# Moving a chain of projections one slot later behind an engine's PSUM read-out, with a per-channel weight folded into a scan's input

## Chip, cores and metric

One NeuronCore of a Trainium2 chip runs the whole program. The metric is device time in microseconds (us) of one execution; the kernel before was timed three times (median 1166.73 us, 1166.54 to 1167.99) and once more under the hardware profiler.

## What is computed

Input x is 8 samples of 512 tokens by 256 channels. Each sample goes through two residual layers.

Layer 0, per sample (all scans run over the tokens, from state 0):

```python
ctx   = ema(x, tau_ctx)                                  # h = alpha*h + x_t
wg    = sigmoid(concat(x, ctx) @ Wg.T + bg);  gated = x * wg
mod   = 0.5 + sigmoid(gelu(x @ Wn1.T + bn1) @ Wn2.T + bn2)      # 8 values a token
traces_d = ema(gated * mod[..., d], tau_d)               # d = 0..7
temporal = sum_d traces_d * blend_w[d]                   # blend_w: 8 x 256, a softmax over d
gate  = sigmoid(temporal @ Wtemp.T + btemp);  soma = gelu(x @ Wsoma.T + bsoma)
x     = x + layernorm((soma * gate) @ Wout.T) * gamma + beta
```

Layer 1 is a mixture: three shared feed-forward networks (256 to 1024 to 256 with relu) and two expert networks picked by a type index, added with weights from a small gate, and the residual.

## The kernel before

**Slots.** Activations are kept as 128 channels by 512 tokens, two tiles for 256 channels. Every fp32 product is three matmuls of rounded and remainder parts (lines 588 to 592). The work of a sample's mixture is 5 networks of 8 hidden tiles, 40 *slots*. In slot k TensorE does `up(k+2)` (6 matmuls, one hidden tile two slots ahead), then `down(k)` (6 matmuls, that tile's share of the network's output in the two banks `ps_down`). ScalarE does `relu(k+2)` (`hid_hi`, line 864), VectorE `relu_lo(k+2)` (`hid_lo`, line 1068). `down(k)` waits for `hid_lo` of tile k. When a network ends (slots 8, 16, 24, 32) ScalarE reads `ps_down` out first (`read_out`, lines 866 to 877, two ACTIVATEs to `y`), and the first `down` of the next network waits for it.

**Beside the mixture** of sample b, layer 0 of sample b+1 is computed. Which step stands where is written by hand in `PLAN_TENSOR`, `PLAN_SCALAR`, `PLAN_VECTOR` and `PLAN_SYNC` (lines 47 to 67): a step at slot k is issued ahead of that slot's mixture work on its engine, a step at k + 0.5 behind it; so on one engine k + 0.5 and k + 1 are the same place, if the step there is alone. Each engine works through its queue in order; semaphores tie the queues together. The plans are for mixtures 0 to 6 (mixture 0 has its own plan up to slot 7); mixture 7 has no layer 0 beside it.

**The traces** are on VectorE. `ema_in{d}` (slot 7.5 + 2d, lines 1157 to 1172) writes `trace = (modb + 0.5) * gates` for both channel tiles and scans tile 0; `ema_out{d}` (slot 8.5 + 2d, lines 1173 to 1185) scans tile 1 and adds both, times `blend_w`, to `temporal` (for d = 0 a TENSOR_SCALAR writes `temporal`). The last, `ema_out7`, is at slot 22.5.

**The context chain behind them**: `temp_hi` on ScalarE (slot 23.5, waits for the last sum) and `temp_lo` on VectorE (24) split `temporal`; `tgate` is 12 matmuls on TensorE (24.5) and two sigmoids on ScalarE (25); `sg`, `sg_hi`, `sg_lo` multiply by `soma` and split; `out` is 24 short matmuls (27.5); `ln_stats`, `ln_sqrt`, `ln_norm` normalize; `turn` transposes on TensorE (31.5) and ScalarE reads it out (32.5); `x2`, `x2_hi`, `x2_lo` (33 to 34.5) make the next mixture's input. SyncE loads the next x into `xt` at slot 33, once `x2` has used the old one.

**Others.** `mod` is a sigmoid of 8 x 512 on ScalarE (line 916) with a `nop` behind it that raises `mod_ready`; SyncE stores it to DRAM and loads it back as a broadcast (`modb`). `shared_gate_part` is six VectorE instructions of 256 elements at slot 33 (`GATE_PART_SLOT`). In mixture 0 and a few slots of mixture 1, weights are still being split: ScalarE rounds (`wi_round`, `wo_round`, `tile_round`, line 833), GpSimd subtracts (lines 1473, 1478, 1484), SyncE loads and stores the parts (`load_tile`, `keep_tile`, lines 450 to 462), all in the order of the same slots.

```python
                elif step == "temp_hi":
                    act.wait_ge(ema_sum, (n - 1) * (2 * D) + 2 * D)
                    hi(both(ct_hi), both(temporal)).then_inc(temp_hi_ready, 1)
```

Of the kernel before, what the change touches and what calls it, by code (L numbers as in the profile page):

```python
# [7 lines left out]
ALU = mybir.AluOpType  # L8
ACT = mybir.ActivationFunctionType
# [5 lines left out]
P = 128  # L15
B, T, E = 8, 512, 256
CT = E // P
D = 8
# [27 lines left out]

PLAN_TENSOR = {
    0.5: ["mod_hidden"], 1.5: ["soma"], 2.5: ["mod", "gate_hidden"], 4.5: ["wgate"],
    24.5: ["tgate"], 27.5: ["out"], 31.5: ["turn"],
}  # L50
PLAN_SCALAR = {
    1: ["mod_hidden"], 2: ["soma"], 3: ["mod"], 4: ["gate_exp"], 5: ["wgate"],
    23.5: ["temp_hi"], 25: ["tgate"], 26: ["sg_hi"], 29: ["ln_sqrt"], 32.5: ["turn"], 34: ["x2_hi"],
    36: ["next_x_hi"], 38.5: ["next_ctx_hi"],
}
PLAN_VECTOR = {
    0.5: ["gate_part"], 1.5: ["mod_hidden_lo"], 3.5: ["gate_logits"],
    4.5: ["gate_soft", "mix1", "mix2"], 5.5: ["mix3"], 6: ["gated"], 6.5: ["mix0"],
    24: ["temp_lo"], 25.5: ["sg"], 26: ["sg_lo"], 28.5: ["ln_stats"], 29.5: ["ln_norm"], 33: ["x2"], 34.5: ["x2_lo"],
    36.5: ["next_x_lo"], 37: ["next_ctx_scan"], 39: ["next_ctx_lo"],  # L60
}
for _d in range(D):
    PLAN_VECTOR[7.5 + 2 * _d] = [f"ema_in{_d}"]
    PLAN_VECTOR[8.5 + 2 * _d] = [f"ema_out{_d}"]
PLAN_SYNC = {
    3: ["mod"], 4: ["modb0", "modb1"], 8: ["store"], 10: ["modb2"], 14: ["modb3"], 33: ["next_x"],
}
PLANS = {"sync": PLAN_SYNC, "tensor": PLAN_TENSOR, "scalar": PLAN_SCALAR, "vector": PLAN_VECTOR, "gpsimd": {}}

# [18 lines left out]
FILLERS = {"x": 10, "out": 3, "normed1": 2, "x2": 7, "gate": 5, "mix": 20}  # L88
OPEN_SPREAD = 2
OPEN_VECTOR_INPUTS = {0: 0, 1: 1, 4: 3, 6: 5}  # L90
GATE_PART_SLOT = 33
MIX_ORDER = (1, 2, 3, 0)
HALF = T // 2
FINAL_OWN = P
# [39 lines left out]
def build(nc, x, w_ctx, params, types_row, types_all, shared_wi, shared_wo, expert_wi, expert_wo,  # L134
# [5 lines left out]
    with ExitStack() as ctx:  # L140
# [3 lines left out]
        def sem(name):  # L144
            return ctx.enter_context(nc.semaphore(name))
# [38 lines left out]
        mod = sb("mod", [D, T])  # L184
        modb = sb("modb", [P, 2, 2, T])
# [3 lines left out]
        alpha = sb("alpha", [P, D + 1])  # L189
        blend_w = sb("blend_w", [P, CT, D])  # L190
# [71 lines left out]
        mod_ready = sem("mod_ready")  # L262
# [568 lines left out]
        def _(act):  # L831
# [62 lines left out]
            def beside(step, k, p):  # L894
                n, f = p.n, p.f
                if step in ("x_hi", "next_x_hi"):
                    m = n + (step == "next_x_hi")
                    act.wait_ge(x_loaded, m * 16 + 16)
                    hi(both(xg_hi), both(xt)).then_inc(x_hi_ready, 1)
                elif step in ("ctx_hi", "next_ctx_hi"):  # L900
                    m = n + (step == "next_ctx_hi")
                    act.wait_ge(ctx_ready, m * 2 + 2)
                    hi(both(ct_hi), both(ctxt)).then_inc(ctx_hi_ready, 1)
                elif step == "soma":
                    for c in range(CT):
                        act.wait_ge(aux_ready[c], p.aux[c]["soma"] + 1)
                        act.activation(soma[:, c, :], ps_aux[c][:, :], ACT.Gelu, bias=col(C_BSOMA, c))\
                            .then_inc(aux_free[c], 1)
                elif step == "mod_hidden":
                    act.wait_ge(aux_ready[0], p.aux[0]["mod_hidden"] + 1)  # L910
                    act.activation(modh[:, :], ps_aux[0][:, :], ACT.Gelu, bias=col(C_BN1)).then_inc(aux_free[0], 1)
                    act.wait_ge(aux_free[0], p.aux[0]["mod_hidden"] + 1)
                    hi(modh_hi[:, :], modh[:, :]).then_inc(modh_hi_ready, 1)
                elif step == "mod":
                    act.wait_ge(aux_ready[1], p.aux[1]["mod"] + 1)
                    act.activation(mod[:, :], ps_aux[1][0:D, :], ACT.Sigmoid, bias=par[0:D, C_BN2:C_BN2 + 1])\
                        .then_inc(aux_free[1], 1)
                    act.wait_ge(aux_free[1], p.aux[1]["mod"] + 1)
                    act.nop().then_inc(mod_ready, 1)
                elif step in ("wgate", "tgate"):  # L920
                    bias = {"wgate": C_BG, "tgate": C_BTEMP}[step]
                    for c in range(CT):
                        act.wait_ge(aux_ready[c], p.aux[c][step] + 1)
                        act.activation(gates[:, c, :], ps_aux[c][:, :], ACT.Sigmoid, bias=col(bias, c))\  # L924
                            .then_inc(aux_free[c], 1)
# [3 lines that stand above are left out]
                elif step == "sg_hi":  # L929
                    act.wait_ge(sg_ready, (n - 1) * 2 + 2)  # L930
                    hi(both(xg_hi), both(gates)).then_inc(sg_hi_ready, 1)
                elif step == "ln_sqrt":
                    act.wait_ge(meanvar_ready, n)
                    act.activation(std[:, :], meanvar[:, :, 1], ACT.Sqrt, bias=eps[:, :]).then_inc(std_ready, 1)
                elif step == "turn":

                    if later((n - 1) * 16):
                        act.wait_ge(out_stored, (n - 1) * 16)
                    for c in range(CT):
                        act.wait_ge(aux_ready[c], p.aux[c]["turn"] + 1)  # L940
# [117 lines left out]
        def _(dve):  # L1058
# [38 lines left out]
            def mixture(b, k, parity, last):  # L1097
# [22 lines left out]
            def final_mix(parity):  # L1120
# [10 lines left out]
                dve.tensor_tensor(x2[:, parity, 1, FINAL_OWN:T], ps_aux[1][:, FINAL_OWN:T], x2[:, parity, 1, FINAL_OWN:T],  # L1131
                                  ALU.add).then_inc(final_added, 1)

            def beside(step, k, p):
                n, f = p.n, p.f
                if step in ("x_lo", "next_x_lo"):
# [20 lines left out]
                elif step.startswith("ema_in"):  # L1157

                    d = int(step[-1])
# [4 lines left out]
                    for c in range(CT):  # L1164
                        if d:

                            dve.wait_ge(ema_sum, (n - 1) * (2 * D) + (2 * d - 1 + c))
                        dve.scalar_tensor_tensor(trace[:, c, :], modb[:, d // 2 % 2, d % 2, :], 0.5, gates[:, c, :],  # L1168
                                                 ALU.add, ALU.mult).then_inc(ema_in, 1)
                    dve.wait_ge(ema_in, (n - 1) * (2 * D) + (2 * d + 1))  # L1170
                    dve.tensor_tensor_scan(trace[:, 0, :], alpha[:, d:d + 1].broadcast_to([P, T]), trace[:, 0, :], 0.0,  # L1171
                                           ALU.mult, ALU.add).then_inc(ema_trace, 1)
                elif step.startswith("ema_out"):
                    d = int(step[-1])
                    dve.wait_ge(ema_in, (n - 1) * (2 * D) + (2 * d + 2))
                    dve.tensor_tensor_scan(trace[:, 1, :], alpha[:, d:d + 1].broadcast_to([P, T]), trace[:, 1, :], 0.0,  # L1176
                                           ALU.mult, ALU.add).then_inc(ema_trace, 1)
                    for c in range(CT):
                        dve.wait_ge(ema_trace, (n - 1) * (2 * D) + (2 * d + 1 + c))
                        if d == 0:  # L1180
                            last = dve.tensor_scalar(temporal[:, c, :], trace[:, c, :], blend_w[:, c, 0:1], None, ALU.mult)
                        else:
                            last = dve.scalar_tensor_tensor(temporal[:, c, :], trace[:, c, :], blend_w[:, c, d:d + 1],  # L1183
                                                            temporal[:, c, :], ALU.mult, ALU.add)
                        last.then_inc(ema_sum, 1)
                elif step == "temp_lo":
                    dve.wait_ge(temp_hi_ready, n)
                    lo(both(ct_lo), both(temporal), both(ct_hi)).then_inc(temp_split, 1)
# [7 lines left out]
                elif step == "ln_stats":  # L1196
# [6 lines left out]
                    for t in range(TT):  # L1203
                        last = dve.bn_aggr(meanvar[:, t, :], stats[:, t, :])
# [386 lines left out]
```

## Time and profile before

| | |
|---|---|
| median of 3 runs | 1166.73 us |
| the profiled execution's own time | 1168.23 us |
| its span (first to last instruction) | 1166.2 us |
| TensorE busy | 1093.4 us, 94% |
| VectorE busy | 798.5 us, 68% |
| ScalarE busy | 410.6 us, 35% |
| GpSimd busy | 121.0 us, 10% |
| mean granted TensorE clock | 0.969 of full |

PE is TensorE, DVE VectorE, ACT ScalarE, POOL GpSimd, SPq the queue on which SyncE issues DMAs. In rows of the timeline the first number is the start in us from the span's start, the second the time from the start to the end of the piece, "x2" the instructions merged in it, and a bracket the idle time of the engine before it with what ended it. A row of a group by form has its busy time in us and the mean of one in ns. Busy time of PE holds overlap (a matmul of 512 columns shows about 0.39 us and the next starts 0.23 us after it), so what TensorE loses is read from starts and waits, not from the share.

### The profile page before, as it was taken

The page shows a single profiled execution, that of the slowest core. Times are in us where ns is not written, and L with a number is a line of the kernel's source. Part 1 is how long each engine was busy: PE and PEld are TensorE (multiplying, and loading weights), DVE is VectorE, ACT ScalarE, POOL GpSimd, SP SyncE. Part 2 cuts the span into 40 slices and gives each one's busy share as a digit, 9 for nine tenths or more (in the row PEclk, how much of TensorE's full clock was granted, in tenths as well). Part 3 has the DMA queues.
Part 4 walks back from the last instruction along what each step waited for, and adds up shares of the span by engine and source line. Part 5 has one row for each costly group of instructions (what it writes and reads, how often), then busy time and mean ns, then how long its engine had stood idle before and what let it go on. Part 6 is the DMA issues. An engine that isn't in the chain of part 4 may idle for free.

```text
span 1166.2 us, 12367 instructions
## 1 busy us (share of the span) xinstructions
PE 1093.4 (94%) x4706; PEld 869.8 (75%) x4706; DVE 798.5 (68%) x1223; ACT 410.6 (35%) x638; POOL 121.0 (10%) x50
## 2 busy tenths in 40 slices
PE   7699677989889999999999999999999999999998
PEld 5177456768678887888878887788878888788886
DVE  7975996638965589465975589465975589545225
ACT  7155333643224422343233422343233422332221
POOL 2814445512000000000000000000000000000000
PEclk9599988989999999999999999999999999999999
DMA  5058794478835546354645456354644465455550
GB/s 213 5 198 291 282 347 150 179 285 279 311 136 194 181 181 234 112 201 181 230 144 198 180 182 219 124 198 173 243 145 164 176 218 201 144 180 199 206 179 30
DMA packets 37772, 224.30 MB, mean 192 GB/s; under 512 B 4498, under 2 KB 4754, under 8 KB 16082
## 3 DMA queue, kind: packets, MB, share of 16 engines
q1 hardware_dynamic: 37714, 223.52, 53.2%
q8 instruction: 37, 0.61, 0.2%
q14 instruction: 21, 0.17, 0.0%
HBM read 189.82 MB, written 33.69 MB: 192 GB/s over the span
## 4 chain that ended last, share of the span: by engine, by line
PE 59%; DVE 33%; DMA 3%; issue 2%; ACT 2%; SPq 0%; DVEq 0%; ACTq 0%
PE ps_down L590 8%; PE ps_up L590 8%; PE ps_down L592 8%; PE ps_up L592 8%; PE ps_up L591 8%; PE ps_down L591 8%; DVE trace L1168 6%; DVE temporal L1183 5%; DVE hid_lo L1068 5%; DVE trace L1176 5%; DVE trace L1171 5%; PE ps_aux L590 3%; PE ps_aux L591 3%; PE ps_aux L592 3%; DMA split_wi<-ex 2%
## 5 line engine op out<-in xcount | busy, mean ns | idle before, releaser
L1068 DVE SCALAR_TENSOR_TENSOR hid_lo<-ps_up,hid_hi 128x512 fp32r<-128x512 f32 x320 | 219.5, 687 | 330.8 <-ACT hid_hi L864 329.5
L864 ACT ACTIVATE hid_hi<-ps_up 128x512 fp32r<-128x512 f32 x320 | 191.6, 599 | 495.7 <-PE ps_up L592 495.4
L590 PE MATMUL ps_down<-hid_hi,wo 128*128 128x512 f32 x640 | 257.7, 403 | 40.4 <-ACT y L876 22.7
L590 PE MATMUL ps_up<-x_hi,wi 128*128 128x512 f32 (+1 forms) x644 | 257.1, 399 | 3.0 <-DMA wi<-split_wi 2.9
L592 PE MATMUL ps_down<-hid_hi,wo 128*128 128x512 f32 x640 | 254.5, 398 | 0.0
L592 PE MATMUL ps_up<-x_hi,wi 128*128 128x512 f32 (+1 forms) x644 | 253.2, 393 | 0.0
L591 PE MATMUL ps_up<-x_lo,wi 128*128 128x512 f32 (+1 forms) x644 | 253.2, 393 | 0.0
L591 PE MATMUL ps_down<-hid_lo,wo 128*128 128x512 f32 x640 | 251.4, 393 | 0.0
L590 PEld LDWEIGHTS ps_down<-hid_hi,wo 128*128 128x128 f32 x640 | 120.9, 189 | 74.2 <-issue 30.0
L590 PEld LDWEIGHTS ps_up<-x_hi,wi 128*128 128x128 f32 x644 | 121.5, 189 | 30.5 <-DMA wi<-split_wi 3.8
L592 PEld LDWEIGHTS ps_down<-hid_hi,wo 128*128 128x128 f32 x640 | 121.2, 189 | 29.8
L592 PEld LDWEIGHTS ps_up<-x_hi,wi 128*128 128x128 f32 x644 | 122.2, 190 | 28.4
L591 PEld LDWEIGHTS ps_down<-hid_lo,wo 128*128 128x128 f32 x640 | 121.5, 190 | 27.7
L591 PEld LDWEIGHTS ps_up<-x_lo,wi 128*128 128x128 f32 x644 | 122.0, 189 | 26.5
L1183 DVE SCALAR_TENSOR_TENSOR temporal<-trace,blend_w,temporal 128x512 f32<-128x512 f32 x98 | 82.9, 891 | 0.0
L1168 DVE SCALAR_TENSOR_TENSOR trace<-modb,gates 128x512 f32<-128x512 f32 x112 | 77.2, 733 | 0.0
L1176 DVE TENSOR_TENSOR_SCAN trace<-alpha,trace 128x512 f32<-128x512 f32 x56 | 73.4, 1310 | 0.0
L1171 DVE TENSOR_TENSOR_SCAN trace<-alpha,trace 128x512 f32<-128x512 f32 x56 | 70.7, 1262 | 0.0
L1484 POOL TENSOR_TENSOR ex<-ex 128x1024 fp32r<-128x1024 f32 x16 | 41.5, 2597 | 79.2 <-ACT ex L833 79.2
L1117 DVE SCALAR_TENSOR_TENSOR x<-y,g,x 128x512 f32<-128x512 f32 x56 | 41.0, 785 | 0.2
L924 ACT ACTIVATE gates<-ps_aux,par 128x512 f32<-128x512 f32 x28 | 19.3, 689 | 61.5 <-PE ps_aux L592 61.5
L1478 POOL TENSOR_TENSOR wo<-raw_wo,wo 128x1024 fp32r<-128x1024 f32 x10 | 27.7, 2771 | 55.2 <-ACT wo L833 55.2
(197 smaller groups left out, 1004.3 us busy)
## 6 DMA issues: line engine op xcount, KB each, us to landing
wi<-split_wi SPq DMA_DIRECT2D x70, 1024.0 KB, 4.9
wo<-split_wo SPq DMA_DIRECT2D x70, 1024.0 KB, 4.8
modb<-mod_scratch SPq DMA_DIRECT2D x28, 512.0 KB, 4.5
split_wi<-ex SPq DMA_DIRECT2D x8, 1024.0 KB, 8.7
split_wo<-ex SPq DMA_DIRECT2D x8, 1024.0 KB, 9.3
split_wi<-wi SPq DMA_DIRECT2D x6, 1024.0 KB, 7.5
split_wo<-wo SPq DMA_DIRECT2D x6, 1024.0 KB, 8.3
xt<-in_x SPq DMA_DIRECT2D x8, 512.0 KB, 3.6
```

The source lines that it names most:

```text
L590: pe.matmul(ps, w_hi, x_hi, start=start, stop=False)
L591: pe.matmul(ps, w_hi, x_lo, start=False, stop=False)
L592: return pe.matmul(ps, w_lo, x_hi, start=False, stop=stop)
L864: act.activation(hid_hi[:, k % NU, :], ps_up[k % NU][:, :], ACT.Relu).then_inc(hid_hi_ready, 1)
L1068: dve.scalar_tensor_tensor(hid_lo[:, k % NU, :], ps_up[k % NU][:, :], 0.0, f32(hid_hi[:, k % NU, :]), ALU.max, ALU.subtract).then_inc(hid_ ...
L1117: dve.scalar_tensor_tensor(x2[:, parity, c, :], y[:, y_at(i, parity), c, :], g[:, i:i + 1], x2[:, parity, c, :], ALU.mult, ALU.add).then_i ...
L1168: dve.scalar_tensor_tensor(trace[:, c, :], modb[:, d // 2 % 2, d % 2, :], 0.5, gates[:, c, :], ALU.add, ALU.mult).then_inc(ema_in, 1)
L1171: dve.tensor_tensor_scan(trace[:, 0, :], alpha[:, d:d + 1].broadcast_to([P, T]), trace[:, 0, :], 0.0, ALU.mult, ALU.add).then_inc(ema_trac ...
L1176: dve.tensor_tensor_scan(trace[:, 1, :], alpha[:, d:d + 1].broadcast_to([P, T]), trace[:, 1, :], 0.0, ALU.mult, ALU.add).then_inc(ema_trac ...
L1183: last = dve.scalar_tensor_tensor(temporal[:, c, :], trace[:, c, :], blend_w[:, c, d:d + 1], temporal[:, c, :], ALU.mult, ALU.add)
L1478: pool.tensor_tensor(wo_lo[:, u % 2, :], raw_wo[:, u % 2, :], f32(wo_hi[:, u % 2, :]), ALU.subtract)\
L1484: pool.tensor_tensor(ex[:, j % 2, 1, :].bitcast(F32R), ex[:, j % 2, 1, :], ex[:, j % 2, 0, :], ALU.subtract)\
```

## The change

- The chain from `temp_hi` to `x2_lo` is moved back by a half to a whole slot in the four plans; `next_x` by one slot; `GATE_PART_SLOT` from 33 to 31.
- The 0.5 is added to `mod` by a second ScalarE instruction (in place of the `nop`); `ema_in` multiplies `modb` by the column of `blend_w` and by `gates`, so that what is scanned is already weighted.
- `ema_out` adds by TENSOR_TENSOR. For d = 0 the product is written into `temporal` and scanned there, and the two TENSOR_SCALARs are gone.

```diff
-    24.5: ["tgate"], 27.5: ["out"], 31.5: ["turn"],
+    25.5: ["tgate"], 28.5: ["out"], 32: ["turn"],
 PLAN_SCALAR
-    23.5: ["temp_hi"], 25: ["tgate"], 26: ["sg_hi"], 29: ["ln_sqrt"], 32.5: ["turn"], 34: ["x2_hi"],
+    24.5: ["temp_hi"], 26: ["tgate"], 27: ["sg_hi"], 29.5: ["ln_sqrt"], 33: ["turn"], 34.5: ["x2_hi"],
 PLAN_VECTOR
-    24: ["temp_lo"], 25.5: ["sg"], 26: ["sg_lo"], 28.5: ["ln_stats"], 29.5: ["ln_norm"], 33: ["x2"], 34.5: ["x2_lo"],
+    24.5: ["temp_lo"], 26.5: ["sg"], 27: ["sg_lo"], 29: ["ln_stats"], 30: ["ln_norm"], 33.5: ["x2"], 35: ["x2_lo"],
 PLAN_SYNC
-    3: ["mod"], 4: ["modb0", "modb1"], 8: ["store"], 10: ["modb2"], 14: ["modb3"], 33: ["next_x"],
+    3: ["mod"], 4: ["modb0", "modb1"], 8: ["store"], 10: ["modb2"], 14: ["modb3"], 34: ["next_x"],
-GATE_PART_SLOT = 33
+GATE_PART_SLOT = 31
-                    act.nop().then_inc(mod_ready, 1)
+                    act.activation(mod[:, :], mod[:, :], ACT.Copy, bias=0.5).then_inc(mod_ready, 1)
+            def trace_of(d):
+                return trace if d else temporal
+            def ema_scan(n, d, c):
+                dve.wait_ge(ema_in, (n - 1) * (2 * D) + (2 * d + 1 + c))
+                scan = dve.tensor_tensor_scan(trace_of(d)[:, c, :], alpha[:, d:d + 1].broadcast_to([P, T]), trace_of(d)[:, c, :],
+                                              0.0, ALU.mult, ALU.add)
+                scan.then_inc(ema_trace if d else ema_sum, 1)
-                        dve.scalar_tensor_tensor(trace[:, c, :], modb[:, d // 2 % 2, d % 2, :], 0.5, gates[:, c, :],
-                                                 ALU.add, ALU.mult).then_inc(ema_in, 1)
+                        dve.scalar_tensor_tensor(trace_of(d)[:, c, :], modb[:, d // 2 % 2, d % 2, :], blend_w[:, c, d:d + 1],
+                                                 gates[:, c, :], ALU.mult, ALU.mult).then_inc(ema_in, 1)
 ema_out
-                        if d == 0:
-                            last = dve.tensor_scalar(temporal[:, c, :], trace[:, c, :], blend_w[:, c, 0:1], None, ALU.mult)
-                        else:
-                            last = dve.scalar_tensor_tensor(temporal[:, c, :], trace[:, c, :], blend_w[:, c, d:d + 1],
-                                                            temporal[:, c, :], ALU.mult, ALU.add)
-                        last.then_inc(ema_sum, 1)
+                    ema_scan(n, d, 1)
+                    if d:
+                        for c in range(CT):
+                            dve.wait_ge(ema_trace, (n - 1) * (2 * D - 2) + (2 * d - 1 + c))
+                            dve.tensor_tensor(temporal[:, c, :], trace[:, c, :], temporal[:, c, :], ALU.add).then_inc(ema_sum, 1)
```

## Rows read from the trace of the kernel before

**Rows 1.** What TensorE waited for: us in total, times, longest.

```profile
PE ps_down L590 <- ACT y L876: 22.7, 7, 6.4
PE ps_down L590 <- DVE hid_lo L1068: 16.5, 8, 3.9
...
PE ps_aux L590 <- ACT modh L911: 4.0, 1, 4.0
```

**Rows 2.** Timeline of ScalarE around slot 24 of mixture 2.

```profile
464.67 1.06 ACT L833 ACTIVATE ct_hi<-temporal 128x1024 fp32r<-128x1024 f32 x1 [3.02 <-DVE temporal L1183]
465.64 1.07 ACT L876 ACTIVATE y<-ps_down 128x512 f32<-128x512 f32 x2
```

**Rows 3.** Timeline of VectorE, same stretch.

```profile
459.19 1.29 DVE L1168 SCALAR_TENSOR_TENSOR trace<-modb,gates 128x512 f32<-128x512 f32 x2
...
463.24 1.40 DVE L1183 SCALAR_TENSOR_TENSOR temporal<-trace,blend_w,temporal 128x512 f32<-128x512 f32 x2
464.55 0.69 DVE L1068 SCALAR_TENSOR_TENSOR hid_lo<-ps_up,hid_hi 128x512 fp32r<-128x512 f32 x1
465.76 1.23 DVE L1060 TENSOR_TENSOR ct_lo<-temporal,ct_hi 128x1024 fp32r<-128x1024 f32 x1 [0.52 <-ACT ct_hi L833]
```

**Rows 4.** Timeline of TensorE, same stretch: the first matmul of down in slot 24.

```profile
466.36 0.47 PE L590 MATMUL ps_down<-hid_hi,wo 128*128 128x512 f32 x1 [2.56 <-ACT y L876]
```

**Rows 5.** Stretches after waits: window, its length, busy time of engines, PEclk (granted clock), DMA.

```profile
187.00:191.40 4.40, 4.40 (x12) 3.39 (x12) 0.36 (x1) 0.68 (x2) 2.37 (x1) 0.52 0.09 15
250.00:256.30 6.30, 6.30 (x15) 4.97 (x16) 1.29 (x2) 2.47 (x4) 0.37 (x1) 0.52 0.94 307
334.00:338.40 4.40, 4.40 (x13) 3.47 (x13) 1.14 (x2) 0.65 (x2) 0.00 (x0) 0.61 0.01 4
467.00:471.00 4.00, 4.00 (x13) 3.11 (x12) 0.69 (x1) 0.50 (x2) 0.00 (x0) 0.59 0.00 0
...
731.00:734.00 3.00, 3.00 (x8) 2.32 (x8) 0.41 (x1) 0.00 (x0) 0.00 (x0) 0.51 0.00 0
864.00:868.00 4.00, 4.00 (x13) 3.12 (x12) 0.00 (x0) 0.69 (x1) 0.00 (x0) 0.62 0.00 0
```

**Rows 6.** Groups by form: VectorE's sum with a column, ScalarE's mod.

```profile
L1183 DVE SCALAR_TENSOR_TENSOR temporal<-trace,blend_w,temporal 128x512 f32<-128x512 f32 x98 | 82.9, 891 | 0.0
...
L916 ACT ACTIVATE mod<-ps_aux,par 8x512 f32<-8x512 f32 x7 | 4.8, 680 | 1.2 <-PE ps_aux L647 0.4
```

**Rows 7.** Timeline of ScalarE, tile 11 of mixture 2.

```profile
422.23 0.60 ACT L864 ACTIVATE hid_hi<-ps_up 128x512 fp32r<-128x512 f32 x1 [2.17 <-PE ps_up L592]
```

**Rows 8.** Timeline of VectorE, tile 11 of mixture 2.

```profile
422.86 0.69 DVE L1068 SCALAR_TENSOR_TENSOR hid_lo<-ps_up,hid_hi 128x512 fp32r<-128x512 f32 x1
```

**Rows 9.** Timeline of VectorE in mixture 0, traces 0 and 1, and slot 23.

```profile
118.22 2.98 DVE L1181 TENSOR_SCALAR temporal<-trace,blend_w 128x512 f32<-128x512 f32 x2
...
121.73 2.86 DVE L1168 SCALAR_TENSOR_TENSOR trace<-modb,gates 128x512 f32<-128x512 f32 x2
...
184.01 0.68 DVE L1068 SCALAR_TENSOR_TENSOR hid_lo<-ps_up,hid_hi 128x512 fp32r<-128x512 f32 x1
```

**Rows 10.** Timeline of GpSimd in mixture 0, beside traces 0 and 1.

```profile
118.44 2.48 POOL L1473 TENSOR_TENSOR wi<-raw_wi,wi 128x1024 fp32r<-128x1024 f32 x1 [2.94 <-ACT wi L833]
```

**Rows 11.** Timeline of the DMA queue of SyncE, late in mixture 0.

```profile
223.31 0.43 SPq L461 DMA_DIRECT2D split_wi<-ex  x1
```

**Rows 12.** Timeline of ScalarE, slot 0 of mixture 1.

```profile
246.89 1.06 ACT L833 ACTIVATE ex<-ex 128x1024 fp32r<-128x1024 f32 x1 [5.76 <-DMA ex<-in_expert_wo]
```

**Rows 13.** Timeline of TensorE, mixture 2: down(31) and the turn.

```profile
492.88 0.40 PE L590 MATMUL ps_down<-hid_hi,wo 128*128 128x512 f32 x1
...
494.27 1.03 PE L707 MATMUL ps_aux<-ident,normed 128*128 128x128 f32 x8
```

**Rows 14.** Timeline of VectorE, mixture 2: the normalization.

```profile
489.49 1.90 DVE L1211 TENSOR_SCALAR normed<-ps_aux,meanvar,rstd 128x256 f32<-128x256 f32 x4
```

**Rows 15.** DMA issues: KB each, median us from issue to landing.

```profile
xt<-in_x SPq DMA_DIRECT2D x8, 512.0 KB, 3.6
```

More of the change, by code:

```diff
@@ L1167, in beside @@
                             dve.wait_ge(ema_sum, (n - 1) * (2 * D) + (2 * d - 1 + c))
-                        dve.scalar_tensor_tensor(trace[:, c, :], modb[:, d // 2 % 2, d % 2, :], 0.5, gates[:, c, :],
-                                                 ALU.add, ALU.mult).then_inc(ema_in, 1)
-                    dve.wait_ge(ema_in, (n - 1) * (2 * D) + (2 * d + 1))
-                    dve.tensor_tensor_scan(trace[:, 0, :], alpha[:, d:d + 1].broadcast_to([P, T]), trace[:, 0, :], 0.0,
-                                           ALU.mult, ALU.add).then_inc(ema_trace, 1)
+                        dve.scalar_tensor_tensor(trace_of(d)[:, c, :], modb[:, d // 2 % 2, d % 2, :], blend_w[:, c, d:d + 1],
+                                                 gates[:, c, :], ALU.mult, ALU.mult).then_inc(ema_in, 1)
+                    ema_scan(n, d, 0)
                 elif step.startswith("ema_out"):
                     d = int(step[-1])
[L1175 to L1179, printed above, removed]
-                        if d == 0:
-                            last = dve.tensor_scalar(temporal[:, c, :], trace[:, c, :], blend_w[:, c, 0:1], None, ALU.mult)
-                        else:
-                            last = dve.scalar_tensor_tensor(temporal[:, c, :], trace[:, c, :], blend_w[:, c, d:d + 1],
-                                                            temporal[:, c, :], ALU.mult, ALU.add)
-                        last.then_inc(ema_sum, 1)
+                    ema_scan(n, d, 1)
[3 more added lines that the diff above has]
+                            dve.tensor_tensor(temporal[:, c, :], trace[:, c, :], temporal[:, c, :], ALU.add).then_inc(ema_sum, 1)
                 elif step == "temp_lo":
```

## Prediction

> **What bounds the kernel now.** I read the page first: TensorE is busy nearly all the time and nothing else comes close, so a change that leaves its instructions alone, as this one does, can only give back time in which TensorE waits or runs at the lower clock. Next the list of TensorE's waits [rows 1]. After the opening it has two large entries: 22.7 us in 7 waits for ScalarE's read-out (line 876), and 16.5 us in 8 waits for `hid_lo`. Seven waits, one per mixture with a layer 0 beside it, point to one place. The timelines of mixture 2 show it. VectorE ends the last sum at 464.6 [rows 3]. ScalarE starts `temp_hi` at 464.67 after idling 3.02 us, and only then the read-out at 465.64 [rows 2]; TensorE's down(24) starts at 466.36, 2.56 us of idle time late [rows 4]. The read-out itself could have run long before: `down(23)` had ended. It stood behind a step in ScalarE's queue that waits for VectorE. That is the wait the change goes at.
>
> Two more losses hang on waits. Behind the read-out wait the granted clock is at or near the 1.2 GHz level for a stretch: shares 0.52, 0.61, 0.59, 0.51 and 0.62 [rows 5]. Window length times (1 - share) gives 2.1, 1.7, 1.6, 1.5 and 1.5 us; the engine had just idled 2.5 us or more. (The list has five read-outs of seven; behind the other two the clock did not fall.) And one wait of 4.0 us for `modh` [rows 1], in slot 1 of mixture 1, is followed by 6.3 us at 0.52, 3.0 us lost.
>
> **The change part by part.**
>
> *Read-out, mixtures 1 to 6.* With `temp_hi` at 24.5 ScalarE goes read-out, relu(26), `temp_hi`. All six waits go: 22.7 - 6.4 = 16.3 us idle, and 0.17 us each because idle time is counted from a matmul's end (it shows 0.40 us where the next could start after 0.23 [rows 13]): down(24) starts 2.73 us late, at 466.36 for 463.63. 17.3 us. The clock stretches of three of these mixtures and of mixture 1 add 1.7 + 1.6 + 1.5 + 1.5 = 6.3 us, if no other wait of that size takes their place.
>
> *What is late next.* A slot is 12 matmuls, 2.77 us: six of them lie between 492.88 and 494.27 [rows 13]. So down(25) would start at 466.40. Its `hid_lo` (VectorE, 464.55 + 0.69 = 465.2) is in time by 1.2 us. `tgate` stands behind down(25), at 467.79. Its input: `temp_hi` from 464.67 to 465.73, `temp_lo` 1.23 us after that, 467.1 at the latest with relu_lo(26) ahead of it. In time by 0.7 us. Then `sg` to `sg_lo` have moved by as much as `out`, one slot; nothing changes there.
>
> *Layer norm.* `out` moves by a slot, `turn` does not: 31.5 and 32 are one place on TensorE. The chain between them loses 2.77 us. Counted from the end of `out`, E: up(31) and relu(31) take ScalarE to E + 2.2, a table load and the square root to about E + 3.8, and the normalization's 1.90 us [rows 14] to E + 6.0. `turn` comes three slots after E, at E + 8.3. In time by 2.3 us. `x2`, `x2_hi` and `x2_lo` have three slots of room before up(0) of the next mixture needs them.
>
> *VectorE's work.* Per sample 16 products get a column instead of 0.5, 14 sums lose one, 2 TENSOR_SCALARs go. The trace has no such product. Bounds for one: nothing; and 0.891 us (the mean of the sum with a column, POOL's disturbances in it [rows 6]) less the 0.645 that a product takes now (half of 1.29), 0.25 us. I take 0.06, from the undisturbed pairs beside each other: 1.40 with a column, 1.29 without [rows 3]. The sums, now without one, give back as much: +0.9 - 0.8 = 0.1 us. The two TENSOR_SCALARs gain nothing in steady mixtures: hid_lo(11) behind them starts at 422.86, right as its `hid_hi` ends (422.23 + 0.60) [rows 7, 8]; without them VectorE waits for that. So the last sum stays at 464.6 or 464.7, and the 1.2 and 0.7 us of room above cover it.
>
> *Mixture 0.* Its read-out wait is the longest, 6.4 us (6.6 with refill). Here hid_lo(25) starts at 184.01 and ends at 184.7 [rows 9], and down(25), 2.8 us earlier than that without waits, will wait for it: 6.6 - 2.8 = 3.8 us gained. Behind a wait of 2.8 us the clock fell about every second time: half of 2.1, 1.0 us.
> For the TENSOR_SCALARs in mixture 0 the row shows 2.98 us for two [rows 9], against GpSimd's instruction from 118.44 to 120.92 [rows 10]: the second started under it and ended behind it. What follows them, the product of trace 1, would now start at about 118.9, under the same GpSimd instruction, and end behind it. So 0.5 us (bounds: 0 and 3.0, the whole row).
> The Trainium skill says why (SBUF — State Buffer, "SBUF: two separate sides"): VectorE and GpSimd share a port pair as an exclusive lock, held for a whole instruction, and the loser blocks. By the row alone one would book 3.0 us; by the rule the removed stall passes to the next instruction with two SBUF inputs, and the gain is 0.5.
>
> *Queue of SyncE.* `next_x` at 34 leaves `keep_tile(8)` of slot 33 ahead of it; now that store is issued at 223.31 [rows 11], behind a wait for `x2`. The tile loads of mixture 1 hang on these stores: at 246.89 ScalarE gets a tile after 5.76 us [rows 12], and `modh` behind it is what TensorE waits 4.0 us for. The store chain ahead of it should run 2 to 4 us earlier. Bounds: nothing, and the whole 4.0 + 3.0 us with its clock; I take half, 3.5.
> In steady mixtures `next_x` waits for an `x2` that is one relu_lo later, and the weight load of slot 34 waits behind it, some 2.8 us; x lands 3.6 us after issue [rows 15] and is needed two slots on; both transfers have over 4 us to spare. Costed at nothing.
>
> *Rest.* The added ScalarE instruction is 8 x 512 like `mod`'s own, 0.68 us [rows 6]; `modb` is needed four slots later, and the weight load behind it in SyncE's queue a slot or more. The gate part (under 3 us) moves from a full place on VectorE to an idle one. Nothing for either; without cover they'd cost 0.7 and 2.9 us per sample.
>
> **Sum.** 17.3 + 6.3 + 3.8 + 1.0 + 0.5 + 3.5 = 32.4 us. The profiled execution took 1168.2 us (2.0 more than its span); less 32.4 that is 1135.8. It stands 1.5 us above the median of the runs, so for the median: **1134.3 us**.
>
> **Rivals.**
>
> *VectorE stays the late one.* The wait moves to down(25) and `tgate`. This needs a product dearer than its 0.06: at the upper bound 16 x 0.25 = 4.0 us per sample, less 0.7 of room, 3.3 us times 6 = 20 us given back; at half of that 1.3 x 6 = 8 us. For it: VectorE has no gap from slot 9 on. Against it: the pairs in rows 3. About 12 us: 1146.
>
> *The early mixtures give nothing.* 3.8 + 1.0 + 0.5 + 3.5 = 8.8 us stay, because each stall passes to the next instruction under GpSimd, and the tile loads stay as late. For it: 16.5 us of `hid_lo` waits that the change doesn't touch. 1143.
>
> *They give all.* The `modh` wait and its clock stretch go whole (+3.5), the clock of mixture 0 too, and the earlier stores calm two later waits: 1127.
>
> *Slower.* The layer norm chain, a slot shorter, misses `turn`, on TensorE before slot 32, seven times. It pays once the chain is 2.3 us later than above, and it turns the sign at 2.3 + 32.4/7 = 6.9 us. At 8 us late it is 5.7 x 7 = 40 us lost against 32 won: 1175 for this one. It would take a ScalarE step two slots late. Near break-even the same mechanism makes the change nil, and the read-out gain, though real, isn't seen.
>
> **How the numbers follow.** Forecast 0.60 (own range 1128 to 1141), VectorE late 0.13, early mixtures nothing 0.13, all 0.07, slower or nil 0.07. The likeliest gives 1134.3. The range reaches to 1146 and past the lower rival for the unknowns of the early mixtures: 1125 to 1147. A measurement of this kernel tells about 0.2% (2.3 us) from nothing. All but the last case are faster by far more: faster 0.93, same 0.03, slower 0.04.
>
> **What would show it.** Right: the entry of line 876 gone or down to one in TensorE's waits; in steady mixtures down(24) on its pace, ScalarE's order read-out, relu, `ct_hi`; a pair of products at 1.4 us; mean granted clock up from 0.969; the time between equal slots of two steady mixtures shorter by 2.7 to 4.3 us. Wrong: waits of TensorE for `ct_lo` or for `normed`; more than 16.5 us for `hid_lo` in mixtures 2 to 6; the `modh` wait longer than 4.0 us.

## The result, and the profile after

| | before | after |
|---|---|---|
| median (lowest to highest) | 1167.14 us (1166.54 to 1167.99, 4 runs) | 1136.67 us (1135.93 to 1137.84, 4 runs) |
| the profiled execution's own time | 1168.23 us | 1135.94 us |
| its span | 1166.2 us | 1133.9 us |
| mean granted TensorE clock | 0.969 | 0.978 |

The ratio is 0.9739 with a 95% interval of 0.9722 to 0.9756: 2.6% faster, 30.5 us. The forecast was 1134.3 us in a range of 1125 to 1147. The median lies 2.4 us above the forecast.

TensorE's instructions are the same, so what moved is its waiting. The list of TensorE's waits in the kernel after (us in total, times, longest) answers to [rows 1]:

```profile
PE ps_down L590 <- DVE hid_lo L1068: 13.6, 5, 4.2
...
PE ps_aux L590 <- ACT modh L911: 3.6, 1, 3.6
...
PE ps_aux L590 <- DVE ct_lo L1060: 2.5, 2, 1.5
...
PE ps_down L590 <- ACT y L876: 0.6, 1, 0.6
```

The entry of line 876 had 22.7 us in 7 waits; what is left of it is one wait of 0.6 us, in mixture 0. The two waits for `ct_lo` are not in mixtures 2 to 6 either. The entry for `hid_lo` has not grown, and the one for `modh` is still there. Slot 24 of mixture 2 shows the new order, first on ScalarE (start, duration; answers to [rows 2]):

```profile
448.91 1.09 ACT L876 ACTIVATE y<-ps_down 128x512 f32<-128x512 f32 x2 [0.79 <-PE ps_down L592]
450.29 0.60 ACT L864 ACTIVATE hid_hi<-ps_up 128x512 fp32r<-128x512 f32 x1 [0.29 <-PE ps_up L592]
451.13 1.06 ACT L833 ACTIVATE ct_hi<-temporal 128x1024 fp32r<-128x1024 f32 x1 [0.24 <-DVE temporal L1187]
```

The read-out now waits for `ps_down`, the thing it reads, and not behind a rounding that waits for VectorE. The same stretch on VectorE (answers to [rows 3]), then on TensorE (to [rows 4]: the first matmuls of down(24), down(25) and `tgate`):

```profile
449.84 1.26 DVE L1187 TENSOR_TENSOR temporal<-trace,temporal 128x512 f32<-128x512 f32 x2
451.02 1.28 DVE L1068 SCALAR_TENSOR_TENSOR hid_lo<-ps_up,hid_hi 128x512 fp32r<-128x512 f32 x2
452.23 1.23 DVE L1060 TENSOR_TENSOR ct_lo<-temporal,ct_hi 128x1024 fp32r<-128x1024 f32 x1
```

```profile
450.09 0.40 PE L590 MATMUL ps_down<-hid_hi,wo 128*128 128x512 f32 x1
...
452.87 0.40 PE L590 MATMUL ps_down<-hid_hi,wo 128*128 128x512 f32 x1
...
454.25 0.40 PE L590 MATMUL ps_aux<-ct_hi,wc_hi 128*128 128x512 f32 x1
```

None of the three has a bracket, so none waited. `ct_lo` ends at 452.23 + 1.23 = 453.46, 0.8 us ahead of `tgate`.

**Where the 32.3 us came from.** Take as a mixture's length the time from the first matmul of down(0) to that of the next mixture. Mixture 2 runs from 386.18 to 518.72 before and from 372.65 to 500.80 after. The timeline of TensorE in the kernel after:

```profile
372.65 0.40 PE L590 MATMUL ps_down<-hid_hi,wo 128*128 128x512 f32 x1
...
500.80 0.40 PE L590 MATMUL ps_down<-hid_hi,wo 128*128 128x512 f32 x1
```

Read in this way from each profiled execution (us; "steady" are mixtures 2 to 6):

| kernel | mixture 0 | mixture 1 | steady mixtures |
|---|---|---|---|
| before | 157.95 | 145.85 | 132.54, 130.95, 132.55, 132.56, 130.95 |
| after | 151.22 | 138.99 | 128.15 to 128.17 |
| won | 6.7 | 6.9 | 18.7 in all |

The rest (the opening up to down(0), mixture 7 and the end) is equal within 0.1 us.

### The profile page after: what moved, and what is told of

It reads as the page before. It is cut to its first block, busy times and chain, and to the rows that moved or that the text cites. A ratio compares the mean times of both kernels' runs of the same rounds, so it can differ in the third digit from the quotient of the medians.

```text
span 1133.9 us, 12353 instructions
## 1 busy us (share of the span) xinstructions
PE 1081.6 (95%) x4706; PEld 863.4 (76%) x4706; DVE 795.3 (70%) x1209; ACT 417.8 (37%) x645; POOL 120.6 (11%) x50
## 4 chain that ended last, share of the span: by engine, by line
PE 80%; DVE 12%; DMA 5%; ACT 1%; issue 1%; SPq 0%; POOL 0%; DVEq 0%; ACTq 0%
PE ps_up L590 12%; PE ps_down L590 11%; PE ps_up L592 11%; PE ps_up L591 11%; PE ps_down L592 11%; PE ps_down L591 11%; PE ps_aux L590 3%; PE ps_aux L592 3%; PE ps_aux L591 3%; DMA split_wi<-ex 2%; DVE trace L1140 2%; DVE trace L1178 2%; DVE temporal L1187 1%; DMA ex<-in_expert_wo 1%; DVE hid_lo L1068 1%
## 5 line engine op out<-in xcount | busy, mean ns | idle before, releaser
L590 PEld LDWEIGHTS ps_up<-x_hi,wi 128*128 128x128 f32 x644 | 121.9, 189 | 30.5 <-DMA wi<-split_wi 3.6
L1140 DVE TENSOR_TENSOR_SCAN trace<-alpha,trace 128x512 f32<-128x512 f32 x98 | 123.5, 1260 | 0.0
L1178 DVE SCALAR_TENSOR_TENSOR trace<-modb,blend_w,gates 128x512 f32<-128x512 f32 x98 | 78.3, 839 | 0.0
L1187 DVE TENSOR_TENSOR temporal<-trace,temporal 128x512 f32<-128x512 f32 x98 | 74.9, 804 | 0.0
L876 ACT ACTIVATE y<-ps_down 128x512 f32<-128x512 f32 x48 | 26.1, 596 | 23.2 <-PE ps_down L592 23.2
```

The source lines that it names most:

```text
L590: pe.matmul(ps, w_hi, x_hi, start=start, stop=False)
L876: act.activation(y[:, y_at((ffn + 1) % (NS + 1), parity), c, :], ps_down[c][:, :], ACT.Copy, scale=scale)\
L1140: scan = dve.tensor_tensor_scan(trace_of(d)[:, c, :], alpha[:, d:d + 1].broadcast_to([P, T]), trace_of(d)[:, c, :], 0.0, ALU.mult, ALU.add)
L1178: dve.scalar_tensor_tensor(trace_of(d)[:, c, :], modb[:, d // 2 % 2, d % 2, :], blend_w[:, c, d:d + 1], gates[:, c, :], ALU.mult, ALU.mult ...
L1187: dve.tensor_tensor(temporal[:, c, :], trace[:, c, :], temporal[:, c, :], ALU.add).then_inc(ema_sum, 1)
```

## The experiments

Twelve more runs were made, one of them the kernel after once more. Lengths of mixtures come from each one's profiled execution; ratios are against the kernel before, timed beside it.

**1. Each half alone.** `plans_only` is the kernel before with the new plans and `GATE_PART_SLOT = 31`; `fold_only` is the kernel after with the old ones.

```diff
 plans_only, against before:
-    23.5: ["temp_hi"], 25: ["tgate"], 26: ["sg_hi"], ...
+    24.5: ["temp_hi"], 26: ["tgate"], 27: ["sg_hi"], ...
 (and the other lines of the four plans)
 fold_only, against after: the same lines the other way
```

> The kernel before with only the new slots (the four plans and the gate part), without the fold. Theory (the moved wait is the gain): each steady mixture 128.2 us from down(0) to down(0) as in the changed kernel, no wait of TensorE for line 876 beyond 1 us, time 1136 to 1139 us, the rest being mixture 0. Rival (the fold's VectorE work carries the gain): above 1145 us, with waits of TensorE for hid_lo or ct_lo in steady mixtures.

> The changed kernel with the slots of before: only the fold is done. Theory: the read-out wait of 2.6 us per mixture stays, TensorE waits for line 876 about 22 us in 7 times, the time is 1164 to 1167 us (0.5 to 3 us won in mixture 0, where GpSimd is beside). Rival (VectorE's work carries the gain): under 1155 us, with the wait for line 876 under 15 us.

`plans_only` took 1140.37 us (1139.39 to 1141.31), ratio 0.9769 (0.9735 to 0.9803). Its steady mixtures take 128.15 to 128.17 us, exactly as after. `fold_only` took 1165.32 us (1162.89 to 1168.84), ratio 0.9975 (0.9959 to 0.9991), with mixtures 2 to 6 at 130.95 or 132.5 as before and the wait in its place. In its list of waits:

```profile
PE ps_down L590 <- ACT y L876: 23.3, 7, 7.1
```

So the plans carry all of the steady gain. The fold gives 1 to 5 us of its own, some 3, and none of it in mixtures 2 to 6. (The execution of `fold_only` that was profiled is its slowest of ten, so its trace doesn't show where the 3 us are.)

**2. Is it the order on ScalarE?** `temp_hi_early` is the kernel after with one step moved back to where it stood:

```diff
-    24.5: ["temp_hi"], 26: ["tgate"], ...
+    23.5: ["temp_hi"], 26: ["tgate"], ...
```

> The changed kernel with the one ScalarE step temp_hi back at slot 23.5, ahead of the read-out; all else stays moved. Theory (ScalarE's queue order is the cause): the wait for line 876 is back, 7 times, about 2.6 us in steady mixtures, with stretches of lower clock behind some; 1160 to 1167 us. Rival (having tgate and the rest later is the cause): under 1145 us.

1164.07 us (1160.98 to 1167.78), ratio 0.9970 (0.9944 to 0.9996). One step at its old place in the plan takes back almost everything. Its list of waits, and the first matmul of down(24) in mixture 2:

```profile
PE ps_down L590 <- ACT y L876: 17.9, 8, 3.3
```

```profile
460.42 0.47 PE L590 MATMUL ps_down<-hid_hi,wo 128*128 128x512 f32 x1 [2.57 <-ACT y L876]
```

It is the wait of [rows 4] again, 2.57 us for 2.56, with the folded product in place. The steady mixtures take 132.54, 130.97, 132.55, 132.60 and 130.97 us.

**3. Is moving `temp_hi` alone enough?** `split_only` is the kernel before with only `temp_hi` and `temp_lo` at 24.5; `tgate` and all behind it stay.

```diff
-    23.5: ["temp_hi"], 25: ["tgate"], ...
+    24.5: ["temp_hi"], 25: ["tgate"], ...
-    24: ["temp_lo"], ...
+    24.5: ["temp_lo"], ...
```

> The kernel before with only temp_hi and temp_lo moved to slot 24.5; tgate stays at 24.5 on TensorE. Theory: the read-out wait is gone, and TensorE waits at tgate for ct_lo instead, about 2.1 us a mixture (467.1 less 465.0 in the times of mixture 2 before), so that most is given back: 1155 to 1163 us. Rival (only the read-out counts, tgate's slot is of no matter): 1136 to 1141 us.

1162.16 us (1160.38 to 1165.06), ratio 0.9940 (0.9919 to 0.9960). The read-out wait is gone, and a new one stands a few matmuls later. The list of waits, then the first matmul of `tgate` in mixture 2:

```profile
PE ps_aux L590 <- DVE ct_lo L1060: 18.1, 8, 3.8
```

```profile
466.09 0.50 PE L590 MATMUL ps_aux<-ct_hi,wc_hi 128*128 128x512 f32 x1 [1.86 <-DVE ct_lo L1060]
```

Steady mixtures shrink by 0.7 us only (130.95 to 130.28, 132.55 to 131.9); two of the five are of the longer kind, where the kernel before has three. VectorE's last sum has not moved, so whatever reads it next has to be late by the difference. Only moving the readers too, which gives the chain a slot, removes the wait.

**4. How much room is left on VectorE?** `pad` is the kernel after with six small memsets, each waiting for the last, ahead of trace 7's product.

```diff
+                    if d == D - 1:
+                        for i in range(6):
+                            if (n - 1) * 6 + i > 0:
+                                dve.wait_ge(pad_done, (n - 1) * 6 + i)
+                            dve.memset(pad[:, :], 0.0).then_inc(pad_done, 1)
```

> The changed kernel with six memsets of 128 x 128 on VectorE ahead of the product of trace 7, 1.2 us or a little more a mixture, each behind the one before. Theory (0.8 us of room at tgate, 1.2 at down(25)): TensorE waits for ct_lo about 0.4 us plus what the memsets exceed 1.2 us, in every steady mixture, 128.5 to 129.2 us each; 3 to 6 us slower in all. Rival (VectorE has more room than that): 128.2 us each and no such wait.

1143.80 us (1143.75 to 1143.84), ratio 0.9786 (0.9758 to 0.9815). VectorE and TensorE in mixture 2:

```profile
450.09 1.46 DVE L1180 MEMSET pad<- 128x128 f32 x6
...
457.91 1.23 DVE L1062 TENSOR_TENSOR ct_lo<-temporal,ct_hi 128x1024 fp32r<-128x1024 f32 x1
```

```profile
458.74 0.39 PE L594 MATMUL ps_down<-hid_hi,wo 128*128 128x512 f32 x1
459.19 0.51 PE L592 MATMUL ps_aux<-ct_hi,wc_hi 128*128 128x512 f32 x1
```

`ct_lo` starts 457.91 - 377.01 = 80.90 us into the mixture, in the kernel after 452.23 - 372.65 = 79.58: the memsets put it off by 1.32 us. Each steady mixture gets 0.70 us longer (128.85 for 128.15), so the room was 1.32 - 0.70, about 0.6 us, over all the places where VectorE is waited for. `tgate` is one of them: the last matmul ahead of it starts at 458.74 and `tgate` 0.45 us later, not 0.23, right behind the end of `ct_lo` at 459.14. It starts 459.19 - 377.01 = 82.18 us into the mixture, for 454.25 - 372.65 = 81.60: 0.58 us late, so the room at `tgate` itself was 1.32 - 0.58, over 0.7 us. Some 0.35 us of the delay arose ahead of it, at down(24) and down(25), which use `hid_lo`.

**5. How much room has the layer norm?** `out_late` is the kernel after with `out` a slot later, `turn` unmoved.

```diff
-    25.5: ["tgate"], 28.5: ["out"], 32: ["turn"],
+    25.5: ["tgate"], 29.5: ["out"], 32: ["turn"],
```

> The changed kernel with out at slot 29.5 on TensorE, so that the layer norm chain has one slot (2.77 us) less before the turn. Theory (2.4 us of room): TensorE waits for normed 0.4 to 1.5 us in each of 7 mixtures, 128.5 to 129.7 us per steady mixture. Rival (the chain is nearer to its limit or the slots behind it slip too): over 131 us per steady mixture.

1136.39 us (1136.27 to 1136.50), ratio 0.9723 (0.9695 to 0.9751), steady mixtures 128.15 to 128.17. The wait that I expected did not come, nor did the rival's 131 us. In mixture 2, on ScalarE, VectorE and TensorE:

```profile
468.07 1.28 ACT L934 ACT_TABLE_LOAD   x1
472.80 0.30 ACT L934 ACTIVATE std<-meanvar,eps 128x4 f32<-128x4 f32 x1 [3.44 <-DVE meanvar L1206]
```

```profile
473.46 1.90 DVE L1213 TENSOR_SCALAR normed<-ps_aux,meanvar,rstd 128x256 f32<-128x256 f32 x4
```

```profile
476.92 1.03 PE L707 MATMUL ps_aux<-ident,normed 128*128 128x128 f32 x8
```

`normed` ends at 475.36, and 1.6 us are left. In the kernel after the same rows read:

```profile
472.08 1.90 DVE L1213 TENSOR_SCALAR normed<-ps_aux,meanvar,rstd 128x256 f32<-128x256 f32 x4
```

```profile
476.37 1.03 PE L707 MATMUL ps_aux<-ident,normed 128*128 128x128 f32 x8
```

That is 476.37 - 473.98 = 2.4 us of room. Moving `out` by a slot of 2.77 us used up only 0.8 us of it. The rows of ScalarE tell why: the table load is done at 469.35, and the square root runs as soon as VectorE's statistics are there. Neither a `relu` nor the table load lies between, whereas my chain had both of them behind the end of `out`. The chain's length depends on where it starts, and I had extended it as if it were fixed.

**6. Why did the `modh` wait stay?** Three kernels, the edits all against after: `next_x_33` (the load of x back at slot 33), `next_x_34h` (half a slot later, behind that slot's weight load in SyncE's queue) and `keep_early` (the store of a split tile one slot earlier).

```diff
 next_x_33
-    ... 14: ["modb3"], 34: ["next_x"],
+    ... 14: ["modb3"], 33: ["next_x"],
 next_x_34h
-    ... 14: ["modb3"], 34: ["next_x"],
+    ... 14: ["modb3"], 34.5: ["next_x"],
 keep_early
-                if (j := tile_at(b, k, 9)) is not None:
+                if (j := tile_at(b, k, 8)) is not None:
```

> The changed kernel with next_x back at slot 33 in SyncE's plan. Theory of the prediction (next_x ahead of keep_tile(8) delays the chain of tile stores and loads by 2 to 4 us): in mixture 0 that store is issued only behind the x load, the wait of TensorE for modh grows by about 2 us over the 3.6 of the changed kernel, 1137.5 to 1140 us. Rival (the DMA engines are nearly full from there on, so an earlier store lands no earlier): modh wait and time as in the changed kernel within 1 us. Steady mixtures 128.2 us in both.

> The changed kernel with next_x at slot 34.5, behind the 1 MB weight load of slot 34, which in mixture 0 no longer waits for x2 while the DMA engines are at 0.09 of their time. Theory (the DMA engines' full stretch before slot 0 of mixture 1 sets when tile 11 arrives): the weight load leaves some 4 us sooner, the modh wait falls by 1 to 3 us, 1133 to 1136 us. Rival (the tile chain's own round trip, store landing then load, sets it): modh wait unchanged at 3.6 us, same time.

> The changed kernel with each split tile's store one slot sooner (offset 8 instead of 9). Theory (the round trip of a tile's buffer, store landing then load, is the chain's limit): modh wait smaller by 1 to 3 us, 1132 to 1136 us. Rival (DMA engines full): unchanged, or slower because SyncE waits for GpSimd with weight loads behind it.

| kernel | median us | ratio (interval) | slots 0 and 1 of mixture 1 |
|---|---|---|---|
| before | 1167.14 | 1 | 16.7 us |
| after | 1136.67 | 0.9739 (0.9722 to 0.9756) | 16.2 us |
| next_x_33 | 1139.70 | 0.9751 (0.9726 to 0.9775) | 11.2 us |
| next_x_34h | 1131.17 | 0.9686 (0.9654 to 0.9719) | 9.7 us |
| keep_early | 1136.49 | 0.9724 (0.9704 to 0.9744) | 9.9 us |

The queue of SyncE in the kernel after, late in mixture 0 (issue time, source line; answers to [rows 11]):

```profile
211.83 0.34 SPq L461 DMA_DIRECT2D split_wi<-ex  x1
218.70 0.33 SPq L496 DMA_DIRECT2D xt<-in_x  x1
219.13 0.37 SPq L483 DMA_DIRECT2D wi<-split_wi  x1
219.54 0.43 SPq L455 DMA_DIRECT2D ex<-in_expert_wo  x1
...
221.79 0.44 SPq L461 DMA_DIRECT2D split_wi<-ex  x1
...
233.94 0.33 SPq L455 DMA_DIRECT2D ex<-in_expert_wo  x1
```

And in `next_x_34h`:

```profile
215.98 0.33 SPq L483 DMA_DIRECT2D wi<-split_wi  x1
220.43 0.33 SPq L496 DMA_DIRECT2D xt<-in_x  x1
220.81 0.43 SPq L455 DMA_DIRECT2D ex<-in_expert_wo  x1
...
223.56 0.43 SPq L461 DMA_DIRECT2D split_wi<-ex  x1
...
232.44 0.33 SPq L455 DMA_DIRECT2D ex<-in_expert_wo  x1
```

Take the first matmul of down(0) of mixture 1 as the zero of time: it starts at 240.33 before, at 233.65 after, and at 235.43 in `next_x_34h`. In the kernels before and after:

```profile
240.33 0.40 PE L590 MATMUL ps_down<-hid_hi,wo 128*128 128x512 f32 x1
...
242.66 0.33 SPq L455 DMA_DIRECT2D ex<-in_expert_wo  x1
```

```profile
233.65 0.40 PE L590 MATMUL ps_down<-hid_hi,wo 128*128 128x512 f32 x1
...
239.84 1.06 ACT L833 ACTIVATE ex<-ex 128x1024 fp32r<-128x1024 f32 x1 [5.38 <-DMA ex<-in_expert_wo]
```

The store at 211.83 did go ahead of the load of x, and the chain of tiles did run earlier. Its last load was issued 2.33 us behind down(0) before and 0.29 us (233.94) after: 2.0 us earlier, where the prediction said 2 to 4. But ScalarE got the tile 246.89 - 242.66 = 4.2 us behind that issue before ([rows 12]) and 239.84 - 233.94 = 5.9 us after. So the tile came only 0.4 us earlier, and so did `modh`. Why this load took longer isn't shown. It isn't the queue's order alone: `temp_hi_early` issues the same load as close behind down(0) (238.77 for 238.51), has the tile 4.4 us later, at 243.18, and its `modh` wait is 2.0 us.

What else could be won shows in `next_x_34h`. In the kernel after x waits for `x2`, and until 218.70 the weight load stood behind it, with the DMA engines nearly idle; then everything went out at once. The windows of the kernel after and of `next_x_34h` (the last two columns are the DMA share and GB/s):

```profile
215.00:220.00 5.00, 5.00 (x22) 3.80 (x21) 4.44 (x8) 2.62 (x4) 1.86 (x2) 1.00 0.09 20
```

```profile
216.00:221.00 5.00, 5.00 (x22) 3.78 (x21) 4.96 (x7) 2.65 (x5) 1.86 (x2) 1.00 0.78 280
```

Counted from down(0), the weight load leaves 4.9 us earlier in `next_x_34h`, the tile load 0.5 us. The store that the last load waits for leaves at the same point in both (11.9 us ahead of down(0)), but the load follows it after 232.44 - 223.56 = 8.9 us, where it took 233.94 - 221.79 = 12.1 us after and 242.66 - 230.47 = 12.2 us before. ScalarE idles 1.42 us, and the `modh` wait is gone:

```profile
237.64 1.06 ACT L833 ACTIVATE ex<-ex 128x1024 fp32r<-128x1024 f32 x1 [1.42 <-DMA ex<-in_expert_wo]
```

`next_x_33` was expected to make the `modh` wait longer by 2 us, and did the opposite: 1.2 us. Its time lies in the expected range for another reason. It pays just before, where a weight load comes late:

```profile
232.61 0.77 PE L590 MATMUL ps_up<-x_hi,wi 128*128 128x512 f32 x1 [3.28 <-DMA wi<-split_wi]
```

Mixture 0 takes 160.1 us there, the longest of all. Its interval overlaps that of after, so no gain of the step from 33 to 34 by itself is shown. `keep_early` has no `modh` wait either, but its opening was 4 us longer in the profiled execution, and a weight load comes late in mixture 1 (3.1 us of wait, 1.6 in after); its ratio does not part from after's. `next_x_34h` did better than expected (the whole wait gone, not 1 to 3 us of it). Its interval ends at 0.9719, just below that of after, which begins at 0.9722.

**7. Both cures together.** `next_x_keep` has 34.5 and 8.

> The changed kernel with both: next_x at slot 34.5 behind the weight load, and each split tile's store one slot sooner. Theory (both shorten the tile chain into mixture 1, next_x_34h having taken the modh wait away by itself): as next_x_34h or up to 2 us better, 1129 to 1132 us, no modh wait. Rival (with the DMA engines full an earlier store only pushes the weight loads back): slower than next_x_34h, 1133 us or more, with waits for split_wi or split_wo.

1133.84 us (1132.49 to 1136.08), ratio 0.9704 (0.9683 to 0.9726), mixture 1 at 132.9 us. The 1129 to 1132 us of the theory did not come. It is no better than `next_x_34h` alone: the wait was gone already. The rival's time came, but not its sign: TensorE waits 2.3 us for `split_wi`, 2.8 in after.

**8. How steady is mixture 0?** `after_again` is the kernel after, unchanged, in another session.

> The changed kernel once more, in five rounds, to see how far executions of it lie apart and to stand beside the next run on one chip. Steady mixtures 128.2 us; mixtures 0 and 1 together, 290.2 us in its first profile, may differ by some us between executions, since each of VectorE's instructions there falls against GpSimd's as it comes. Time 1134 to 1139 us; a modh wait of 3 to 4 us if that comes from the order of the DMA queue, another value in each profile if it comes by chance.

1138.89 us (1133.43 to 1140.61), ratio 0.9732 (0.9705 to 0.9760); this interval overlaps that of `next_x_34h` a little, so what carries the case for that version is mixture 1 as well: 132.6 us, against 139.0 and 139.1 in the two profiled executions of after. `next_x_keep`, timed beside `after_again`, is faster too: its median is 5.1 us lower. The steady mixtures repeat to 0.01 us; mixture 0 took 154.98 us and not 151.22. The waits of TensorE around slots 23 to 25 differ between the two. In the kernel after, then in `after_again`:

```profile
176.33 0.50 PE L590 MATMUL ps_down<-hid_hi,wo 128*128 128x512 f32 x1 [4.17 <-DVE hid_lo L1068]
```

```profile
186.15 0.79 PE L590 MATMUL ps_down<-hid_hi,wo 128*128 128x512 f32 x1 [3.88 <-DVE hid_lo L1068]
```

One program, two sequences of stalls. The pair of sums of trace 1 takes 5.57 us in the kernel after (its row stands in the next section), and in `after_again`:

```profile
128.12 1.26 DVE L1187 TENSOR_TENSOR temporal<-trace,temporal 128x512 f32<-128x512 f32 x2
```

Which VectorE instruction meets which GpSimd instruction changes from execution to execution. Nothing below some 4 us can be read from one profiled mixture 0.

**9. Is the fold's gain that of the two TENSOR_SCALARs?** `fold_copy` is the kernel after with trace 0 scanned in its own buffer and copied to `temporal` by two TENSOR_SCALARs.

```diff
-                return trace if d else temporal
+                return trace
...
+                        if d == 0:
+                            last = dve.tensor_scalar(temporal[:, c, :], trace[:, c, :], 1.0, None, ALU.mult)
```

> The changed kernel, but trace 0 goes through the trace buffer again and is copied to the sum by two TENSOR_SCALARs (times 1.0). Theory (what the fold gains lies in the two TENSOR_SCALARs of trace 0, in mixture 0 beside GpSimd): like the changed slots without the fold, 3 us slower than the changed kernel, about 1140 us, mixture 0 from down(0) to down(0) 154 to 155 us against 151.2. Rival (the TENSOR_SCALARs cost 0.5 us as forecast, the rest is how VectorE's and GpSimd's instructions fall against each other): within 1.5 us of the changed kernel. Steady mixtures 128.2 us in both.

1137.85 us (1131.43 to 1140.88), ratio 0.9722 (0.9688 to 0.9756). With the two instructions back the median is 1.2 us above that of after, as the rival said, though the interval is 8 us wide. The instructions are not shown to be the source of what the fold gives, and nor is anything else.

## Why the prediction was right, point by point

- **Read-out wait, mixtures 1 to 6, 17.3 us, and its clock, 6.3 us: right.** For mixtures 2 to 6 the steps give 5 x 2.73 + 1.6 + 1.5 + 1.5 = 18.3 us; 18.7 was measured. `temp_hi_early` brings the wait back by that step alone.
- **What is late next: right.** The room at `tgate` was put at 0.7 us; 0.8 us is in the trace, and `pad` measured over 0.7 there and about 0.6 over all. `split_only` shows what stands there without the moved `tgate`.
- **Layer norm: right in number, wrong in form.** 2.3 us of room forecast, 2.4 measured. But the chain was given as one fixed length after E. `out_late` shows that ScalarE's part lies beside it, not in it, when `out` ends later. So the slower rival, in which each microsecond of delay beyond 2.3 costs one, was priced too high for a late `out`: a whole slot, 2.77 us, cost nothing. What a late step of ScalarE would cost was not run.
- **Product with a column +0.06, sum without -0.06: right.** The sums and products have changed places: the last sum pair takes 1.26 us for the 1.40 of [rows 3], the last product pair, with its column, 1.40 for 1.29. The rival of a dear product is out, and `plans_only` and after share their steady length. The product pair of trace 7 in mixture 2 of the kernel after:

```profile
445.67 1.40 DVE L1178 SCALAR_TENSOR_TENSOR trace<-modb,blend_w,gates 128x512 f32<-128x512 f32 x2
```

- **Mixture 0, 3.8 + 1.0 + 0.5 = 5.3 us: not told apart.** 6.7 us in one profiled execution, 3.0 in another.
- **TENSOR_SCALARs in mixture 0, "0.5 us": open.** The fold as a whole gave 1 to 5 us in `fold_only`, more than the 0.5 booked for it, but `fold_copy` doesn't show these two instructions to be the source. No run isolates that a removed stall passes on to the next instruction with two SBUF inputs. What the trace of after shows is such a stall: the pair of sums of trace 1 in mixture 0, beside GpSimd,

```profile
123.37 5.57 DVE L1187 TENSOR_TENSOR temporal<-trace,temporal 128x512 f32<-128x512 f32 x2
```

```profile
122.33 3.32 POOL L1486 TENSOR_TENSOR ex<-ex 128x1024 fp32r<-128x1024 f32 x1
125.61 2.79 POOL L1480 TENSOR_TENSOR wo<-raw_wo,wo 128x1024 fp32r<-128x1024 f32 x1
```

  where the second sum ends at 128.94, 0.5 us behind GpSimd's end at 128.40. That agrees with the rule of the Trainium skill (SBUF — State Buffer, "SBUF: two separate sides") that one of the two engines holds the shared port pair for a whole instruction and the other blocks. What the rule does not tell is how many such meetings a mixture has.
- **Queue of SyncE, "I take half, 3.5": the step that failed.** That the tile chain would run 2 to 4 us earlier held, at the low end: 2.0 us. That half of the wait and its clock stretch would go with it did not: the last load took 5.9 us for 4.2, and the tile came 0.4 us earlier. The `modh` wait went from 4.0 to 3.6 us, its clock stretch stayed, and slots 0 and 1 of mixture 1 gained 0.5 us for the 3.5. Why the load took longer stays open. Nor does the place of `next_x` ahead of the store set the wait by itself: `next_x_33` has 1.2 us of it. Mixture 1 as a whole gained 6.9 us, where 3.65 + 1.7 for the read-out and its clock and 3.5 here had been booked, 8.9; some 0.9 of the 6.9 are shorter waits at slots 13 and 16 that no term had. `next_x_34h` shows that the gain was there for another place in the queue.

The profiled execution won 32.3 us where the sum said 32.4, and that so small a difference came out is luck: mixture 1 fell 2.0 us short, mixture 0 gave 1.4 more and the steady mixtures 0.4 more. The median misses by 2.4 us because the profiled execution of after is one of its fastest, that of before its slowest.

## What to carry to other kernels

Before moving a step, list what stands behind it in each queue that it passes: a step that waits for a slow engine must not stand ahead of one that is already free to run, on a compute engine or on the queue that issues DMAs. When a reader is late because its input is late, moving it alone only hands the wait to the next reader; the whole chain has to get the slot, and the room at its end is worth measuring by padding. Trust the steady stages to 0.1 us, and ask several executions about any stage in which VectorE and GpSimd meet.

## What was not expected of the hardware

- **Equal waits, unequal clock.** The read-out wait of 2.56 us is followed by the 1.2 GHz level in three steady mixtures of five: 2, 4 and 5 before (132.5 us long, the others 130.95), and 3, 4 and 6 in `fold_only`, where the stretch behind the wait in mixture 2 has a granted clock of 1.00 for the 0.59 of [rows 5]. It isn't tied to a mixture. The clock costs 1.6 us each time. In `split_only` the same happened behind the `ct_lo` wait of 1.9 us in two of the five, mixtures 3 and 6 (a granted clock of 0.57 over some 4 us; 131.9 us long, the others 130.3). In after, with no wait of that size in mixtures 2 to 6, it fell in none.

The window of 4 us behind that wait of 2.57 us in mixture 2 of `fold_only` (the third number from the end is the granted clock):

```profile
467.60:471.60 4.00, 4.00 (x19) 3.29 (x18) 0.70 (x2) 1.11 (x3) 0.00 (x0) 1.00 0.00 0
```

- **A 1 MB store behind a crowd.** In the kernel after, the load that waits for the store of 221.79 was issued 12.1 us behind it; in `next_x_34h` 8.9 us. The DMA engines were full in both stretches. They differ in how much was moved meanwhile: 371 GB/s for 12.1 us is 4.5 MB, 350 GB/s for 9.0 us 3.2 MB. That this sets the time is my reading and not tested; in the kernel before the same trip took 12.2 us with 322 GB/s, 3.9 MB, a DMA share of 0.89. The two windows, of the kernel after and of `next_x_34h`:

```profile
221.80:233.90 12.10, 12.10 (x55) 9.81 (x54) 10.17 (x12) 5.41 (x8) 2.40 (x1) 1.00 0.98 371
```

```profile
223.50:232.50 9.00, 9.00 (x41) 7.31 (x40) 7.12 (x9) 4.64 (x6) 3.10 (x1) 1.00 1.01 350
```
